# Filler products on TensorE in five waits of a two-layer transformer kernel

## The reference

```python
x = x + _layernorm(_L0_attn_ref(_layernorm(x), ...))   # 16 heads of 16, biases, causal
x = x + _layernorm(_L0_ffn_ref(_layernorm(x), ...))    # 32 experts of 192, top 4, and a shared expert
x = x + _layernorm(_L1_attn_ref(_layernorm(x), ...))   # the same with rotary positions
x = x + _layernorm(_L1_ffn_ref(_layernorm(x), ...))    # 32 experts of 176, top 4, at most 128 tokens each
```

## Time and profile before

| | us |
|---|---|
| median of three executions | 749.33 |
| lowest and highest of them | 745.58, 749.74 |
| the profiled execution | 748.95 |
| its span, first to last instruction | 747.2 |
| TensorE busy in the span | 662.8 (89%) |
| VectorE busy in the span | 476.0 (64%) |

### The profile page before, as it was taken

The page is one execution under the profiler, slowest core; times in us unless marked ns, Lnnn a source line. Parts: engine busy times, 40 slices in busy tenths (PEclk is TensorE's granted clock), DMA queues, the critical chain, the costliest instruction groups (busy, mean ns, idle before and its releaser), DMA issues.

```text
span 747.2 us, 13362 instructions
## 1 busy us (share of the span) xinstructions
PE 662.8 (89%) x4292; PEld 431.4 (58%) x4292; DVE 476.0 (64%) x1360; ACT 326.1 (44%) x683; POOL 263.9 (35%) x313
## 2 busy tenths in 40 slices
PE   4988999999668999999975888999998899999991
PEld 2633343435447999999953523344344456999980
DVE  3688888864583444444476798888865685343457
ACT  2554666673134333224422443666664231433322
POOL 4150212111147776444431282112111203677631
PEclk9999999999689999999996989999999999999996
DMA  3533210070019999999680444012000810489762
GB/s 102 158 124 119 76 36 2 1 236 19 29 45 305 339 324 316 296 317 309 231 272 1 120 138 139 16 36 85 2 1 1 271 35 23 144 289 308 243 210 94
DMA packets 60295, 108.60 MB, mean 145 GB/s; under 512 B 11194, under 2 KB 37131, under 8 KB 60100
## 3 DMA queue, kind: packets, MB, share of 16 engines
q1 hardware_dynamic: 52532, 93.86, 38.2%
q0 software_dynamic: 7632, 13.86, 5.6%
q10 hardware_dynamic: 64, 0.03, 0.0%
HBM read 79.98 MB, written 19.79 MB: 134 GB/s over the span
## 4 chain that ended last, share of the span: by engine, by line
PE 66%; DVE 19%; DMA 6%; issue 3%; POOL 2%; ACT 2%; SPq 2%; ACTq 0%; POOLq 0%; DVEq 0%
PE ps L1177 16%; PE ps L1004 9%; PE ps L990 7%; PE ps L922 7%; PE ps L1190 5%; PE ps L1192 5%; PE ps L1036 4%; DVE mx L1664 4%; PE ps L1148 2%; DMA hb<-outs 2%; PE ps L1116 1%; PE ps L877 1%; PE ps L955 1%; SPq L567 1%; PE ps L976 1%
## 5 line engine op out<-in xcount | busy, mean ns | idle before, releaser
L1345 ACT ACTIVATE X<-ps 128x1024 f32<-128x1024 f32 (+1 forms) x192 | 147.5, 810 | 82.3 <-PE ps L990 81.6
L1664 DVE TENSOR_REDUCE mx<-ps 128x1 f32<-128x512 f32 (+3 forms) x208 | 129.5, 674 | 26.9 <-PE ps L922 17.6
L922 PE MATMUL ps<-KA,QA 112*128 112x512 bf16 (+3 forms) x384 | 117.0, 340 | 9.4 <-DVE mx L1664 3.9
L805 POOL DMA_INDIRECT outs<-w_sgu,token x95 | 94.7, 996 | 73.4 <-DVE w_sgu L2036 58.9
L773 POOL TENSOR_SCALAR_AFFINE_SELECT X<-X 128x512 f32<-128x512 f32 x64 | 40.7, 636 | 204.2 <-ACT X L1345 204.2
L2023 DVE TENSOR_TENSOR X<-ps,X 128x128 f32<-128x128 f32 x95 | 27.7, 292 | 116.7 <-ACT X L1462 116.6
L990 PE MATMUL ps<-QA,KA 114*128 114x512 bf16 (+3 forms) x384 | 95.7, 332 | 2.4 <-ACT X L1345 1.2
L1177 PE MATMUL ps<-QA,KA 128*128 x756 | 94.9, 275 | 1.4 <-ACT QA L1451 1.0
L1177 PEld LDWEIGHTS ps<-QA,KA 128*128 128x128 f32 x756 | 92.0, 192 | 3.8 <-issue 2.1
L922 PEld LDWEIGHTS ps<-KA,QA 112*128 112x128 bf16 x384 | 37.0, 98 | 86.6 <-DVE mx L1664 40.9
L797 POOL DMA_INDIRECT V<-token_rows,row_of_slot x64 | 65.6, 1025 | 58.8 <-DVE row_of_slot L1937 33.2
(11 more groups left out here) (311 smaller groups left out, 892.9 us busy)
## 6 DMA issues: line engine op xcount, KB each, us to landing
KA<-in_ex SPq DMA_DIRECT2D x95, 512.0 KB
X<-in_dn SPq DMA_DIRECT2D x95, 64.0 KB
outs<-empty SPq DMA_DIRECT2D x4, 1024.0 KB, 8.0
V<-outs SPq DMA_DIRECT2D x4, 1024.0 KB, 5.6
QA<-X SPq DMA_DIRECT2D x28, 128.0 KB, 2.5
KA<-X SPq DMA_DIRECT2D x28, 128.0 KB, 2.5
QA<-w_sdn SPq DMA_DIRECT2D x28, 128.0 KB, 2.4
KA<-parts_k SPq DMA_DIRECT2D x28, 128.0 KB, 2.5
```

Source lines behind the costliest of these rows:

```text
L805: pool.indirect_dma_start(out=outs[L], out_offset=bass.IndirectOffsetOnAxis(ap=token[L][:, i:i + 1], axis=0), in_=erows[:, g % OUT_RING, : ...
L922: mm = pe.matmul(ps[:, bank, j * w:(j + 1) * w], QA[0:KQ, h, i * P:(i + 1) * P], KA[0:KQ, h, s0:s0 + w], start=True, stop=not diag or mask ...
L1345: nc.scalar.activation(probs[:, st % PB, 2 * p:2 * p + 2, off:CH], ps[:, 4 + 2 * p:6 + 2 * p, off:CH], ACT.Exp, scale=SCALE).then_inc(S(f" ...
L1664: ins = v.tensor_reduce(mx[:, part, i, h0:h0 + nh], ps[:, n % RB, 0:nh * w].rearrange("p (h w) -> p h w", h=nh), AX.X, ALU.max)
```

## The change

TensorE gets a helper that issues n products of `identb` and `before` (128x128 bfloat16, 128 columns) into a PSUM bank that nobody reads before it is written anew. It is called five times: 40 products at the very start, after the wait for `consts`; 20 and 24 in layer 0's middle, the 24 after a wait for "tail0_again"; 36 and 40 ahead of layer 1's front, after waits for "sums0b" and "sums0a_again". The result isn't used.

```diff
@@ def _(pe):
             pe.wait_ge(S("consts"), 1)
 
+            def keep_on(bank, n):
+
+                for _ in range(n):
+                    pe.matmul(ps[:, bank, 0:P], identb[:, :], before[:, :], start=True, stop=True)
+
+            keep_on(7, 40)
+
             def turn_out(tag, n):
...
             for L in range(2):
+                if L == 1:
+                    pe.wait_ge(S("root_in"), ROOTS.index("sums0b") + 1)
+                    keep_on(0, 36)
+                    pe.wait_ge(S("root_in"), ROOTS.index("sums0a_again") + 1)
+                    keep_on(0, 40)
                 transposes(L, 0)
                 transposes(L, 1)
...
                 if L == 0:
                     shared_up(1)
+                    keep_on(7, 20)
+                    pe.wait_ge(S("root_in"), ROOTS.index("tail0_again") + 1)
+                    keep_on(7, 24)
                     unit(("fT", 1, 0))
                     unit(("fT", 1, 1))
                     unit(("logits", 1, 0))
```

## The result

The changed kernel takes 743.32 us (median of 13 executions, 740.67 to 744.59), the kernel before 747.1 (13 executions beside them, 745.47 to 751.36). The ratio is 0.9937, interval 0.9924 to 0.9951: 4.7 us faster by the ratio, 3.8 by the two medians. The forecast was 743.8, a gain of 5.2.

The account below looks back on a forecast made before the run. The end hangs on attention's TensorE and VectorE work and the experts' loop; the change touches three half-clock stretches. 2.5 + 2.7 + 0 = 5.2 us off the profiled 748.95 gave 743.8 us, range 740.3 to 748.0.

Parts of the forecast that it names:

- start: Kernel start, 40 products: half 1's transposes gain 1.27 us and the eight Q/K records 1.20, together 2.5 us.
- middle: Layer 0's middle, 20 and 24 products: the clock holds, transposes gain 0.88 us and logits 1.85, together 2.7 us.
- front: Ahead of layer 1's front, 36 and 40 products: taken as 0 gain, bounds -0.7 and 1.5 us.
- The step: At the start, the clock rises near 11.4 instead of 16.4 us, putting half 0's transposes off the path: 2.5 us.
- the end of these records: At the start, splitting and DMAs into attention wait for the Q/K records' end, so the 2.5 us reach the kernel's end.
- the logits: In layer 0's middle, the logits go from 3.61 to 1.76 us at full clock, a gain of 1.85 us.
- The sign that I had set, a clock of 1.00 from 188 to 197: In layer 0's middle, half 1's logits take about 1.8 us with the granted clock at 1.00 throughout.
- my rival at 745.5: Only layer 0's middle, or its logits, is lost: start 2.5 and transposes 0.9 give 3.4 us; chance 0.18.
- The mechanism I gave for the 0: In layer 1's front, TensorE works only 1.06 of 3.7 us behind the filler, near the idle time that lowered the clock.
- 0.12 us a product at half clock: Cost of one filler product anywhere at half clock, double the 0.06 us at full clock; upper bound 0.23.
- the rival in which it outlasts its wait: Filler still runs when the transposes could start, delaying all three places by 17.3 us in sum: 766 us, chance 0.03.
- The case at 748.3: The clock is up behind the filler but lost before the work: 748.3 us, chance 0.13.

Follow-up runs that it names:

- e6: The changed kernel with its three added waits kept and all 160 products removed: 748.07 against 748.31 us for the kernel before, ratio 1.0003.
- e8: The changed kernel with longer filler in layer 0's middle, plus 28 products in layer 1's middle and 50 at layer 0's lists: 741.65 us, ratio 0.9913.
- e10: The kernel before with only the front's 36 and 40 products and their waits, a repeat of e3: ratio 0.9996.
- e11: The changed kernel measured again without any edit: 744.11 against 747.45 us for the kernel before, ratio 0.9955.
- e3: The kernel before with only the 36 and 40 products ahead of layer 1's front and their waits added: ratio 1.0016.
- e9: The changed kernel without the 36 and 40 products ahead of layer 1's front: 745.12 against 748.31 us for the kernel before, ratio 0.996.
- e7: The kernel before with filler at the start only, 160 products instead of the change's 40: 751.46 us.
- e5: The kernel before with filler at the start only, 20 float32 transposes in place of the 40 products: 748.46 against 748.31 us.

## Why the prediction was right

The total was right, 743.8 against 743.32, and so was the kind of gain: it takes the products, not the waits (e6), and it comes from the clock, place by place. The parts summed from the table, with filler against without:

| | predicted | profiled pair | mean over the traces |
|---|---|---|---|
| start | 2.5 | 1.9 | 1.6 |
| middle | 2.7 | 2.1 | 2.1 |
| front | 0 | 1.4 | 0.9 |
| sum | 5.2 | 5.4 | 4.6 |

**Start.** The step was right: the rise came ahead of the transposes at 10.40 (I had put it near 11.4), half 0's transposes were off the path, and the stretch shortened by 2.4 us in the pair (predicted 2.5). Two things made it less at the end. I wrote that the end of these records goes through to the end; behind them SP's queue of DMA issues stands on the chain, and one slow issue in it took back 0.5 us in the pair. And before's profile lies high: without filler the stretch took 9.03, 8.17, 8.81, 7.63 and 8.89 us in five traces, a mean of 8.51, against 6.64 in all seven with 40 products. To the first row maximum the means are 30.44 us with (seven traces) and 32.05 without (five), which is the table's 1.6. (The eight records of before were counted as three at 0.86 and five at 0.43; that makes 4.73 us, not the row's 4.64, and the sum goes by the 4.64.)

**Middle.** The transposes came out as worked out, 0.88 us predicted, and 1.94 less 1.06 measured. The term that was mis-sized is the logits: I took 1.76 us, the clock holding, and they took 2.39 in the pair, because it fell within them. The sign that I had set, a clock of 1.00 from 188 to 197, did not come about: it is 0.67 in 194 to 196. The middle is 4.47, 4.64, 4.17 and 4.57 us in the four traces with 20 and 24 products, a mean of 4.46 against 6.56. "Or its logits" was a part of my rival at 745.5, and it came about by half. Why the clock fell in them, no row shows: they are products of 32 columns on 128 by 128, and TensorE was busy for all of the 2.00 us from 194 to 196. With 44 and 40 products, and 12 more in the gap ahead of the logits, they take 1.96 us.

**Front.** I took 0, and that failed as a size: the pair shows 1.4 us, with half 1's transposes at 1.09 where the sign that I had set was the old 1.97. The mechanism I gave for the 0, that the clock is lost in the idle times of 1.2 and 1.7 us behind the filler, is what e8, e10 and e11 show; the profiled execution and e3 show the other case. So 36 and 40 products held in two traces of five. Their mean is 6.24 us, against 7.17 for the seven traces without (6.66 to 8.24), hence 0.9. My sum set it against the one trace of 6.71, and took one case where both occur. What decides between them stays open, and the times alone don't show that the front gains (e3, e9, e10).

**Cost of the filler.** 0.12 us a product at half clock was taken, 0.11 measured. No filler delayed the work behind it, and the rival in which it outlasts its wait needed 160 products to come about (e7).

**The case at 748.3.** It was added up from 0.6 us, half of the transposes' gain at the start, and nothing for the middle and the front, with the clock up behind the filler and lost before the work. No run shows that term. In the seven traces with 40 products the start took 6.64 or 6.65 us, against 7.63 to 9.03 in five without; the middle's transposes took 1.06 or 1.07 us in the four traces with 20 and 24; and in e5 the clock rose during float32 transposes, before any product had run. A clock lost between filler and work is what the front shows, in three traces of five (e8, e10, e11).

That the total fits to half a microsecond is in part luck, twice over. The front's 0.9 us that I left out make up for much of the 1.5 that the start and the middle fell short by. And I took the 5.2 us from one execution of 748.95, while the median of thirteen is 747.1; taken from that, the same sum would have given 741.9. The gain itself was forecast as 5.2 us and measured as 3.4 to 4.7.

## What to carry to other kernels

Filler on TensorE paid here where three things came together: the engine waits for microseconds (5.0 at the start, from 5.39 to 10.39, 5.77 in the middle, 10.97 in the front), the chain goes through it right behind the wait, and the filler reaches close to the work (0.56 us ahead of it at the start, 1.29 in the middle). A gap left between filler and work (1.1 to 1.2 us in the front), or between two short pieces of work (1.7 us there), made the gain a matter of the single execution: the front took 5.30 us in two traces and 6.65 to 6.99 in three. With longer filler and a few products in that gap as well (24 in the front, 12 before the logits) the clock held in every trace, two of the front and three of the logits; which of the two additions did it was not tried apart. Count the filler so that it ends before the wait does at the half-clock price, 0.11 us a product here, since what is over delays the work behind it one for one (in e7 the transposes start 6.65 us after the changed kernel's, and the first split 6.3); and don't take the difference of two profiled executions for the effect, when a stretch that the change never touches moves by 1.7 us of its own.

## What the runs showed of the hardware that was not expected

- Float32 transposes alone brought the clock up: in e5 it rose behind twenty of them as filler, within the real sixteen, which took 2.45 us instead of 3.64.
- The same wait in the same kernel may or may not bring the clock down: the changed kernel's front held in its first profile (5.30 us) and not in e11 (6.97), the front alone held in e3 (5.30) and not in e10 (6.99). Layer 1's middle, the same in every kernel without filler there and with 1.8 to 1.9 us of idle time, took 8.83 us in seven traces and 7.13 in five.
- The time to the rise at the start differs too: without filler the stretch from the first transpose to the first split took from 7.63 to 9.03 us in five traces, with 40 products 6.64 or 6.65 in all seven.
